# Block 0: norms in one step ahead of the keys, two key scratch tiles, one mask transfer, row copy on ScalarE, earlier query projections

## The chip, the cores and the metric

The kernel runs on one core of a Trainium2 chip. Five engines work side by side, each in the order of its own instruction list: TensorE (PE; its weight loads are shown as PEld), VectorE (DVE), ScalarE (ACT), GpSimd (POOL) and SyncE (SP), which only issues transfers (DMAs). They wait for one another through semaphores. The metric is device time in microseconds (us): the median of 3 runs of the kernel before is 5856.54 us (5856.24 to 5871.77). One execution was also profiled; it took 5850.62 us, with a span of 5848.7 us from first to last instruction.

## The reference

Eight blocks are added to a residual `x` (16 batches x 56 rows x 128 features). The change touches the first alone, `L0_xcond`: six layers of adaptive norm, rotary self-attention, adaptive norm, rotary cross-attention over a context of 1500 keys per batch, adaptive norm, and MLP:

```python
NL, D, H, DFF = (6, 128, 16, 512)          # 16 heads of 8 features
def _adaln(x, emb, w, b):
    g, be = jnp.split(emb[:, 0, :] @ w.T + b, 2, axis=-1)
    return _ln(x) * (1.0 + g[:, None, :]) + be[:, None, :]
def _attn(q, k, v, mask):
    scores = jnp.einsum('bqhd,bkhd->bhqk', q, k) / np.float32(np.sqrt(HD))
    scores = jnp.where(mask[:, None, None, :], -jnp.inf, scores)
    return jnp.einsum('bhqk,bkhd->bqhd', jax.nn.softmax(scores, axis=-1), v)
```

In cross-attention the queries come from the normed state and are rotated (`_rope`), the keys come from the context `ctx` (16 x 1500 x 128) and are rotated too, and the values come from the context unrotated.

## The kernel before, in words

Block 0 (class `Block0`) is one long software pipeline. A **slot** is one batch of cross-attention in one layer; there are 6 x 16 = 96 of them (`NS`), numbered 0 to 95. A slot has 12 **steps** (`kt`), one for each tile of 125 keys. Eight slots make a **phase** (`ph`), which also carries, beside the cross-attention of its eight batches, the MLP of the previous eight batches and the self-attention of the next eight. I count places in a phase from 0 to 7 (slot number modulo 8); `t` counts its 96 steps. All engines walk over the same slots and steps, and each emits its own part of every step in a fixed order, so the tables of step numbers (`T_NORM`, `T_ROPE`, `T_SELF` and others) set where a piece of work stands in every engine's list.

What a step holds:
- TensorE: two groups of four score matmuls (L1561) of the current slot, each followed by one matmul for the row maxima of the next slot (L1575); every second step the weighted sums of values (L1587); at steps 0, 4, 8 a projection of 500 keys (L1601), at steps 2, 6, 10 four projections of values (L1609); at step 10 a transposition of the row maxima, "rows" (L1638). The first scores of a slot wait for the copy of those rows and for the exponentials of step 11.
- ScalarE: two exponentials (L2067) per step, then the key's first bf16 part ("hi", L1966, steps 2, 6, 10), its second part ("mid", L1970, one step later), the value copies (L1987).
- VectorE: the row maxima (L1940), the first half of a key's rotation (L1821, L1822), the copy of the rows into the query stack (L1837, at step 11), the softmax division (L1800 and four L1808).
- GpSimd: a key's rotation (L2087, L2091, one step after the key's projection), then what is left after "hi" (L2094) and after "mid" (L2097), each one step later. The same for queries at steps 1, 3, 5. It also multiplies out the adaptive norms (L2121, L2124, L2126) in two halves, one per step, after the key's work of that step: the MLP norm at t = 9 and 10, the self norm at t = 19 and 20, the cross norm at t = 67 and 68. These are steps 9 and 10 of place 0, and steps 7 and 8 of places 1 and 5.
- SyncE: per slot three sets of 6 key transfers (L1475), 6 mask transfers (L1483), 6 query transfers (L1493) and the fetch of a context.

The norm multiplies wait for ScalarE's inverse root (L2016), emitted one step earlier. The rotated projections ("rope": PE L1698, then four VectorE instructions L1871 to L1879) stand at t = 23 and 24 (self query and key) and 71 (cross query) on TensorE and one step later in VectorE's list. Both ScalarE's "hi" and GpSimd's work are in-order: an instruction that waits holds everything behind it. The scratch tile `tm` (`key_temp`) exists once, so VectorE's work on a key waits for L2097 of the key before.

## Time and profile before

| | us |
|---|---|
| median of 3 runs (range) | 5856.54 (5856.24 to 5871.77) |
| the profiled execution | 5850.62 |
| its span | 5848.7 |
| PE busy | 5394.6 (92%) |
| DVE busy | 4044.0 (69%) |
| ACT busy | 3144.3 (54%) |
| POOL busy | 2240.2 (38%) |

Busy is the time in which an engine executed. Idle time that matters is that of the engine which bounds the stage; a wait of another engine costs only where the first one waits for it in turn. In the rows below an instruction's group shows its start in us from the span's start, its length, and in brackets the idle time of its engine before it and what ended it. A windows row has the stretch and its length, then for PE, PEld, DVE, ACT and POOL the busy time and in brackets the number of instructions, then PEclk (the granted clock of TensorE as a share of 2.4 GHz), the share of the DMA engines that was busy, and GB/s. A group of instructions shows partitions x elements, how many there were, busy us, mean ns of one, and the idle time before them.

### The profile page before, as it was taken

To read this page: it belongs to the slowest core of one execution; us is meant where nothing else is said; L and a number is where in the kernel's file an instruction comes from. 1 tells how busy PE (TensorE), PEld (TensorE's weight loads), DVE (VectorE), ACT (ScalarE), POOL (GpSimd) and SP (SyncE) were. 2 spreads that over 40 slices of the span, in tenths; PEclk is the share of its full clock that TensorE was granted. 3 is DMA by queue.
4 is the path that set the end of the run, shared out by engine and by line. 5 is a ranking of instruction groups with operands and counts; after the bars stand their busy time and mean duration, and the time that the engine had idled before them with its cause. 6 is when DMAs were issued, how large, how long until landed. Compare 5 with 4: busy or idle time off the path is not lost.

```text
span 5848.7 us, 144909 instructions
## 1 busy us (share of the span) xinstructions
PE 5394.6 (92%) x57797; PEld 4270.3 (73%) x57797; DVE 4044.0 (69%) x8355; ACT 3144.3 (54%) x6405; POOL 2240.2 (38%) x2209
## 2 busy tenths in 40 slices
PE   5899999999999999999978999999699999989998
PEld 4667677676776766767645799998389889947984
DVE  3888887888888888888744377776556666644653
ACT  1566666766666667666644333434334334424764
POOL 4665665666666666666500000000011111075440
PEclk8999999999999999999988999999899999998998
DMA  2776776767767777677810011110100000030000
GB/s 63 118 124 100 122 116 108 122 110 117 120 110 120 112 114 123 103 124 116 119 51 20 22 33 33 38 37 13 41 12 12 17 17 12 12 121 11 2 1 26
DMA packets 440503, 408.12 MB, mean 70 GB/s; under 512 B 125576, under 2 KB 420947, under 8 KB 437787
## 3 DMA queue, kind: packets, MB, share of 16 engines
q1 hardware_dynamic: 439834, 398.85, 39.2%
q8 instruction: 463, 7.59, 0.7%
q14 instruction: 206, 1.68, 0.1%
HBM read 158.00 MB, written 0.46 MB: 27 GB/s over the span
## 4 chain that ended last, share of the span: by engine, by line
PE 61%; POOL 8%; DVE 7%; SPq 7%; issue 6%; DMA 5%; ACT 4%; POOLq 1%; DVEq 1%; ACTq 0%
PE psum L2248 10%; PE psum L2278 10%; PE psum L1575 5%; PE psum L1587 4%; PE psum L1561 4%; SPq L1475 3%; POOL slot_context L3547 3%; DMA l_ctx_v<-in_ctxV 3%; PE psum L1609 3%; PE psum L1723 3%; PE psum L1601 2%; PE psum L416 2%; SPq L1493 2%; PE psum L430 2%; DVE row_max L1940 2%
## 5 line engine op out<-in xcount | busy, mean ns | idle before, releaser
L1940 DVE TENSOR_REDUCE row_max<-psum 112x1 f32<-112x500 f32 x2304 | 1443.5, 670 | 187.4 <-PE psum L1575 172.6
L2067 ACT ACTIVATE weights<-psum 125x448 f32<-125x448 f32 x2304 | 1141.3, 541 | 521.7 <-PE psum L1561 515.2
L1575 PE MATMUL psum<-key_stack,query_stack 97*128 97x500 bf16 x2304 | 875.7, 381 | 107.9 <-DMA query_stack<-query_parts 47.9
L1561 PEld LDWEIGHTS psum<-query_stack,key_stack 121*128 121x128 bf16 x9216 | 654.6, 99 | 370.7 <-issue 184.4
L1561 PE MATMUL psum<-query_stack,key_stack 121*128 121x112 bf16 x9216 | 837.9, 213 | 33.5 <-ACT weights L2067 28.0
L2278 PE MATMUL psum<-l_ctx_v,l_weights 125*128 125x129 f32 x5376 | 638.6, 274 | 1.8 <-ACT l_u L2352 1.8
L2278 PEld LDWEIGHTS psum<-l_ctx_v,l_weights 125*128 125x128 f32 x5376 | 618.3, 191 | 2.5 <-issue 2.5
L1587 PE MATMUL psum<-weights,values 125*17 125x112 f32 x18432 | 554.9, 261 | 0.0
L1587 PEld LDWEIGHTS psum<-weights,values 125*17 125x17 f32 x18432 | 408.9, 97 | 144.8 <-issue 140.4
L2097 POOL TENSOR_TENSOR key_parts<-key_temp,key_parts 128x500 bf16<-128x500 f32 x288 | 327.2, 1136 | 421.5 <-ACT key_parts L1970 421.5
L2087 POOL TENSOR_TENSOR key_temp<-key_temp,rope_sin 128x500 f32<-128x500 f32 x288 | 360.5, 1252 | 282.2 <-DVE key_temp L1821 282.2
L2366 ACT ACTIVATE l_weights<-l_weights 125x1536 f32<-125x1536 f32 x224 | 332.4, 1484 | 236.3 <-DVE l_weights L2410 236.3
L2410 DVE TENSOR_TENSOR l_weights<-psum,l_shift 125x1536 f32<-125x1536 f32 x224 | 392.0, 1750 | 97.5 <-ACT l_shift L2344 97.5
L2418 DVE TENSOR_REDUCE l_tile_max<-psum 125x128 f32<-125x1536 f32 x224 | 393.4, 1756 | 67.1 <-PE psum L2248 66.3
L2094 POOL TENSOR_TENSOR key_temp<-key_temp,key_parts 128x500 f32<-128x500 f32 x288 | 328.4, 1140 | 231.9 <-ACT key_parts L1966 231.8
L2091 POOL TENSOR_TENSOR key_temp<-key_temp 128x500 f32<-128x500 f32 x288 | 358.2, 1244 | 42.5 <-POOL key_temp L2087 1.7
L2248 PE MATMUL psum<-l_q,l_keys 128*125 128x128 f32 x2688 | 372.3, 283 | 0.6 <-ACT l_q L2238 0.6
L2336 ACT ACTIVATE l_w<-psum,l_stat 128x128 f32<-128x128 f32 x224 | 82.4, 368 | 534.3 <-DVE l_stat L2400 534.2
L1575 PEld LDWEIGHTS psum<-key_stack,query_stack 97*128 97x128 bf16 x2304 | 224.4, 97 | 172.8 <-DMA query_stack<-query_parts 68.4
L2248 PEld LDWEIGHTS psum<-l_q,l_keys 128*125 128x125 f32 x2688 | 331.6, 194 | 22.0 <-issue 21.1
L2248 PE MATMUL psum<-l_q,l_ctx_t 128*125 128x128 f32 x2688 | 343.8, 273 | 0.6 <-ACT l_q L2238 0.6
L3042 POOL MEMSET l_weights<- 125x128 f32 x2 | 0.4, 216 | 884.4 <-DVE x_state L796 884.4
(549 smaller groups left out, 10227.5 us busy)
## 6 DMA issues: line engine op xcount, KB each, us to landing
key_stack<-key_parts SPq DMA_DIRECT2D x1728, 125.0 KB, 4.6
ctx_t<-in_ctxT SPq DMA_DIRECT2D x96, 750.0 KB
l_ctx_v<-in_ctxV SPq DMA_DIRECT2D x32, 750.0 KB
query_stack<-query_parts SPq DMA_DIRECT2D x576, 28.0 KB, 3.4
l_ctx_t<-in_ctxT SPq DMA_DIRECT2D x16, 750.0 KB
slot_context<-in_ctxV SPq DMA_DIRECT2D x16, 750.0 KB
key_stack<-ctx_mask_rows SPq DMA_DIRECT2D x576, 3.9 KB
sm_w<-in_sm_w SPq DMA_DIRECT2D x3, 2048.0 KB
```

The costliest lines, as they stand in the source:

```text
L1561: mm = e.matmul(self.k.psum[:, h, (p % 4) * QC:(p % 4 + 1) * QC], ks[:, at:at + 128], q[:, p * QC:(p + 1) * QC])
L1575: e.matmul(self.k.psum[:, 2 + n % 2, 0:500], q[0:ROWS_MAX, p * QC:p * QC + 128], ks[0:ROWS_MAX, p, c * 500:(c + 1) * 500]).then_inc(self.m ...
L1587: mm = e.matmul(self.k.psum[32 * j:32 * j + 17, 5, g * QC:(g + 1) * QC], v[:, kt, p, :], w[:, p * QC:(p + 1) * QC], start=kt == 0 and g == ...
L1940: e.tensor_reduce(self.largest[:, i % PAIRS, i // PAIRS:i // PAIRS + 1], k.psum[0:QC, 2 + i % 2, 0:500], AX.X, ALU.max, negate=True).then_ ...
L2067: e.activation(half(self.p[kt % RING_P], h), self.k.psum[0:KN, h, 0:HALF], ACT.Exp).then_inc(self.exped.sem, 1)
L2087: e.tensor_tensor(tm[:, 1, :], tm[:, 1, :], self.sin[:, c * 500:(c + 1) * 500], ALU.mult).then_inc(self.key_turned_sin.sem, 1)
L2091: e.tensor_tensor(tm[:, 0, :], tm[:, 0, :], tm[:, 1, :], ALU.add).then_inc(self.key_rotated.sem, 1)
L2248: mm = e.matmul(self.scores(i)[:, t, :], self.keys(b)[:, t * KN:(t + 1) * KN], q)
L2278: mm = e.matmul(acc, p[:, t, :], v[:, t, :], start=t == 0, stop=t == self.tiles - 1)
L2366: op = e.activation(p[:, 0:KT, :], p[:, 0:KT, :], ACT.Exp)
L2410: e.tensor_tensor(p[:, 0:KT, :], self.scores(j), shift.unsqueeze(1).broadcast_to([KN, KT, 128]), ALU.add).then_inc(self.shifted.sem, 1)
L2418: e.tensor_reduce(self.most, self.scores(i).rearrange("p t q -> p q t"), AX.X, ALU.max).then_inc(self.max_ready.sem, 1)
```

## The change

Six edits, all in Block 0 (and line numbers below them shift by a few):
1. `T_ROPE`: the query projections move from t = 23 to 22 and from 71 to 70. The key projection stays at 24.
2. Each norm's two halves stand in one step (the first of the two), and ahead of the query's and key's work of that step on GpSimd.
3. `tm` becomes two tiles, and the wait of VectorE moves from the key before to the one before that.
4. The copy of the rows moves from VectorE (its step 11, after the steps' phase work) to ScalarE (start of step 11, ahead of the exponentials).
5. The six mask transfers of a slot become one of 8 x 1500 elements; the mask's rows are made once as 16 x 1500 instead of 96 x 250.
6. Two of every four transpositions of the sums are written 8 columns further left, so that the division is one multiply of 56 x 128 instead of four of 56 x 32.

```diff
-T_UP, T_DOWN, T_ROPE, T_SV = {13: (0, 1, 2, 3)}, 15, {23: 0, 24: 1, 71: 2}, 24
+T_UP, T_DOWN, T_ROPE, T_SV = {13: (0, 1, 2, 3)}, 15, {22: 0, 24: 1, 70: 2}, 24
...
-            for n in range(6):
-                e.dma_start(dst[ROWS:ROWS + 1, :, n * 250:(n + 1) * 250],
-                            self.mask_rows[6 * b + n:6 * b + n + 1, :].unsqueeze(1).broadcast_to(
-                                [1, PAIRS, 250])).then_inc(self.mask_stacked.sem, 16)
+            e.dma_start(dst[ROWS:ROWS + 1, :, :],
+                        self.mask_rows[b:b + 1, :].unsqueeze(1).broadcast_to([1, PAIRS, L])).then_inc(
+                            self.mask_stacked.sem, 16)
...
-        for g in range(2):
-            for h2 in range(2):
...
-                op = e.tensor_tensor(o[:, m * 32:(m + 1) * 32].rearrange("p (j d) -> p j d", j=4), v,
-                                     spread(inv[:, 4 * m:4 * m + 4], 8), ALU.mult)
-        op.then_inc(side.emptied(*key), 1)
+        e.tensor_tensor(o.rearrange("p (m d) -> p m d", d=8), bk.rearrange("p (m c) -> p m c", c=32)[:, :, 1:9],
+                        spread(inv, 8), ALU.mult).then_inc(side.emptied(*key), 1)
...
-            if (b, c) > (0, 0):
-                e.wait_ge(self.key_lo.sem, self.key_lo(b, c) - 1)
+            if (b, c) > (0, 1):
+                e.wait_ge(self.key_lo.sem, self.key_lo(b, c) - 2)
...
-    def rows_vector(self, e, b):
+    def rows_scalar(self, e, b):
...
+        e.activation(self.q_stack[b % 3][ROWS:ROWS_ALL, :].rearrange("r (p c) -> r p c", p=PAIRS),
+                     rows.unsqueeze(1).broadcast_to([1 + 3 * PAIRS, PAIRS, QC]), ACT.Copy).then_inc(
+                         self.side.emptied(*key), 1)
...
@@ gpsimd @@
+                ph, t = s // BH, 12 * (s % BH) + kt
+                for name, at in T_NORM.items():
+                    layer = MLP_OF(ph) if name == "mlp" else NEXT_OF(ph)
+                    if layer is not None and t == at + 3:
+                        for h in range(2):
+                            self.norm_gpsimd(e, name, ph, layer, h)
                 if 0 <= s + 2 < NS:
                     self.query_gpsimd(e, s, kt)
                 self.key_gpsimd(e, s, kt)
-                ph, t = s // BH, 12 * (s % BH) + kt
-                for name, at in T_NORM.items():
-                    layer = MLP_OF(ph) if name == "mlp" else NEXT_OF(ph)
-                    if layer is not None and t - at - 3 in range(2):
-                        self.norm_gpsimd(e, name, ph, layer, t - at - 3)
```

GpSimd's list around an MLP norm (steps 8 to 11 of place 0; `x_normed` rows are the norm, `key_temp` and `key_parts` the key, `query_block` is step 1 of the next slot), before:

```order
L2087 TENSOR_TENSOR key_temp<-key_temp,rope_sin 128x500
L2091 TENSOR_TENSOR key_temp<-key_temp 128x500
L2121 TENSOR_TENSOR x_normed<-ln_deviation 128x224
L2124 TENSOR_TENSOR x_normed<-x_normed,adaln_scale_shift 128x224
L2126 TENSOR_TENSOR x_normed<-x_normed,adaln_scale_shift 128x224
L2094 TENSOR_TENSOR key_temp<-key_temp,key_parts 128x500
L2121 TENSOR_TENSOR x_normed<-ln_deviation 128x224
L2124 TENSOR_TENSOR x_normed<-x_normed,adaln_scale_shift 128x224
L2126 TENSOR_TENSOR x_normed<-x_normed,adaln_scale_shift 128x224
L2097 TENSOR_TENSOR key_parts<-key_temp,key_parts 128x500
L2105 TENSOR_TENSOR query_block<-l_q,head_parity 128x112
```

The same place of the changed kernel:

```order
L2115 TENSOR_TENSOR x_normed<-ln_deviation 128x224
L2118 TENSOR_TENSOR x_normed<-x_normed,adaln_scale_shift 128x224
L2120 TENSOR_TENSOR x_normed<-x_normed,adaln_scale_shift 128x224
L2115 TENSOR_TENSOR x_normed<-ln_deviation 128x224
L2118 TENSOR_TENSOR x_normed<-x_normed,adaln_scale_shift 128x224
L2120 TENSOR_TENSOR x_normed<-x_normed,adaln_scale_shift 128x224
L2081 TENSOR_TENSOR key_temp<-key_temp,rope_sin 128x500
L2085 TENSOR_TENSOR key_temp<-key_temp 128x500
L2088 TENSOR_TENSOR key_temp<-key_temp,key_parts 128x500
L2091 TENSOR_TENSOR key_parts<-key_temp,key_parts 128x500
L2099 TENSOR_TENSOR query_block<-l_q,head_parity 128x112
```

The key's rotation (L2087 and L2091 before, L2081 and L2085 now) stood ahead of the norm and now stands behind all six of its multiplies.

ScalarE's list at the same place (inverse root of the norm, the exponentials `weights` of steps 9 and 10, key hi, values, step 11), before:

```order
L2016 ACTIVATE ln_deviation<-ln_deviation 128x224 x2
L2067 ACTIVATE weights<-psum 125x448 x4
L1966 ACTIVATE key_parts<-key_temp 128x500
L1987 ACTIVATE values<-psum 125x32x16
L2067 ACTIVATE weights<-psum 125x448 x2
L1970 ACTIVATE key_parts<-key_temp 128x500
```

and of the changed kernel:

```order
L2008 ACTIVATE ln_deviation<-ln_deviation 128x224 x2
L2061 ACTIVATE weights<-psum 125x448 x4
L1958 ACTIVATE key_parts<-key_temp 128x500
L1979 ACTIVATE values<-psum 125x32x16
L1830 ACTIVATE query_stack<-psum 25x896
L2061 ACTIVATE weights<-psum 125x448 x2
L1962 ACTIVATE key_parts<-key_temp 128x500
```

The row copy (L1830) stands between the key's and values' copies of step 10 and the exponentials of step 11, in every slot.

TensorE's list from the rows of step 10 to the first scores of the next slot, where a query projection (`l_w_attend`) moves, before:

```order
L1638 MATMUL psum<-ident_bf,neg_max_parts 72x112
L1561 MATMUL psum<-query_stack,key_stack 128x112 x4
L1575 MATMUL psum<-key_stack,query_stack 128x500
L1561 MATMUL psum<-query_stack,key_stack 128x112 x4
L1575 MATMUL psum<-key_stack,query_stack 128x500
L1587 MATMUL psum<-weights,values 17x112 x16
L1698 MATMUL psum<-x_normed,l_w_attend 128x448
L1561 MATMUL psum<-query_stack,key_stack 128x112 x4
```

and of the changed kernel:

```order
L1637 MATMUL psum<-ident_bf,neg_max_parts 72x112
L1697 MATMUL psum<-x_normed,l_w_attend 128x448
L1560 MATMUL psum<-query_stack,key_stack 128x112 x4
L1574 MATMUL psum<-key_stack,query_stack 128x500
L1560 MATMUL psum<-query_stack,key_stack 128x112 x4
L1574 MATMUL psum<-key_stack,query_stack 128x500
L1586 MATMUL psum<-weights,values 17x112 x16
L1560 MATMUL psum<-query_stack,key_stack 128x112 x4
```

The projection moved ahead of step 11's scores and maxima; VectorE's four rope instructions move from ahead of the maxima of the next slot's step 0 to ahead of those of step 11.

## Rows read from the trace of the kernel before

**Rows 1.** Windows: slots 32 and 39 (places 0 and 7)
```profile
1118.44:1142.39 23.95, 23.78 (x358) 16.80 (x354) 21.09 (x47) 18.67 (x41) 16.86 (x18) 1.00 0.91 142
1329.35:1356.13 26.78, 23.90 (x353) 16.98 (x349) 21.18 (x45) 17.69 (x38) 16.01 (x16) 0.94 0.92 143
```

**Rows 2.** Waits of PE in Block 0's slots (total us, times, longest us)
```profile
PE psum L1575 <- DMA query_stack<-query_parts: 45.6, 32, 3.5
PE psum L1575 <- DVE row_max L1940: 29.1, 47, 1.4
PE psum L1561 <- ACT weights L2067: 28.0, 38, 1.0
PE psum L1747 <- DVE query_stack L1837: 7.8, 22, 0.4
```

**Rows 3.** Timeline of ACT at an MLP norm, slot 32
```profile
1137.64 0.67 ACT L2016 ACTIVATE ln_deviation<-ln_deviation 128x224 f32<-128x224 f32 x2
1140.09 0.61 ACT L1966 ACTIVATE key_parts<-key_temp 128x500 bf16<-128x500 f32 x1
1141.23 0.97 ACT L2067 ACTIVATE weights<-psum 125x448 f32<-125x448 f32 x2
```

**Rows 4.** Timeline of POOL there
```profile
1137.03 1.27 POOL L2087 TENSOR_TENSOR key_temp<-key_temp,rope_sin 128x500 f32<-128x500 f32 x1 [1.38 <-DVE key_temp L1821]
```

**Rows 5.** Timeline of PE there: first scores of slot 33
```profile
1142.39 0.37 PE L1561 MATMUL psum<-query_stack,key_stack 121*128 121x112 bf16 x4
```

**Rows 6.** Timeline of POOL at a cross norm, slot 29 (place 5)
```profile
1061.55 0.67 POOL L2121 TENSOR_TENSOR x_normed<-ln_deviation 128x224 f32<-128x224 f32 x1
...
1065.36 1.24 POOL L2087 TENSOR_TENSOR key_temp<-key_temp,rope_sin 128x500 f32<-128x500 f32 x1
```

**Rows 7.** Timeline of ACT there
```profile
1068.03 0.62 ACT L1966 ACTIVATE key_parts<-key_temp 128x500 bf16<-128x500 f32 x1 [3.13 <-POOL key_temp L2091]
```

**Rows 8.** Timeline of PE there: first scores of slot 30, and its second step
```profile
1069.71 0.36 PE L1561 MATMUL psum<-query_stack,key_stack 121*128 121x112 bf16 x4 [0.95 <-ACT weights L2067]
...
1072.29 0.39 PE L1575 MATMUL psum<-key_stack,query_stack 97*128 97x500 bf16 x1 [0.56 <-DVE row_max L1940]
```

**Rows 9.** Timeline of DVE there: rope, then row maxima
```profile
1068.80 0.62 DVE L1871 SCALAR_TENSOR_TENSOR l_q<-psum,rope_cos 128x448 f32<-128x448 f32 x1 [0.38 <-PE psum L1698]
...
1071.56 1.26 DVE L1940 TENSOR_REDUCE row_max<-psum 112x1 f32<-112x500 f32 x2
```

**Rows 10.** Timeline of PE at a late query stack, slot 39
```profile
1351.17 0.38 PE L1575 MATMUL psum<-key_stack,query_stack 97*128 97x500 bf16 x1 [2.82 <-DMA query_stack<-query_parts]
```

**Rows 11.** Windows of PE there: us, PE busy, PEclk, DMA share, GB/s
```profile
1352.00:1356.00 4.00, 4.00 (x51) 0.57 1.12 132
```

**Rows 12.** Windows: slot 7, columns as in rows 1
```profile
382.57:410.93 28.36, 24.75 (x352) 17.66 (x349) 21.53 (x45) 17.69 (x38) 15.69 (x16) 0.88 0.93 144
```

**Rows 13.** Groups by line: copies on DVE and ACT
```profile
L1837 DVE COPY query_stack<-psum 25x896 bf16<-25x896 bf16 x95 | 58.7, 618 | 11.3 <-PE psum L1638 7.9
L1987 ACT ACTIVATE values<-psum 125x512 f32<-125x512 f32 x282 | 166.5, 590 | 11.8 <-PE psum L1609 7.5
L1957 ACT ACTIVATE sums<-psum 128x224 f32<-128x224 f32 x95 | 34.0, 358 | 53.1 <-PE psum L1587 53.1
```

**Rows 14.** Timeline of SP, slot 39: mask, keys, queries
```profile
1334.71 4.10 SPq L1483 DMA_DIRECT2D key_stack<-ctx_mask_rows  x6
1338.85 5.25 SPq L1475 DMA_DIRECT2D key_stack<-key_parts  x6
```

**Rows 15.** Timeline of POOL, slot 39: the key that the second SP row waits for
```profile
1337.45 1.14 POOL L2097 TENSOR_TENSOR key_parts<-key_temp,key_parts 128x500 bf16<-128x500 f32 x1 [0.54 <-ACT key_parts L1970]
```

**Rows 16.** Timeline of POOL at the start: making the masks
```profile
58.30 2.45 POOL L2145 TENSOR_SCALAR src_mask<-src_mask 1x896 bf16<-1x896 uint8 x1
60.82 0.86 POOL L2146 TENSOR_SCALAR ctx_mask_rows<-ctx_mask 96x250 bf16<-96x250 uint8 x1
62.95 3.34 POOL L2163 TENSOR_TENSOR l_qd<-l_q,head_of_feature 128x896 f32<-128x896 f32 x2 [1.27 <-DVE l_q L1879]
```

More of the change, by code:

```diff
@@ L1290, in __init__ @@
             self.q_tmp = sb("query_block", [128, 2, QC])
-            self.tm = sb("key_temp", [128, 2, 500])
+            self.tm = [sb(f"key_temp{i}", [128, 2, 500]) for i in range(2)]
             self.ctx_t = [sb(f"ctx_t{i}", [128, L])[:, :] for i in range(2)]
@@ L1616, in fixed_tensor @@
             for i in range(4):
-                tr = e.transpose(side.bank(*key)[0:S, i * 128:(i + 1) * 128], self.acc[:, i * S:(i + 1) * S],
-                                 k.ident[:, :])
+                at = i * 128 - 8 * (i % 2)
+                tr = e.transpose(side.bank(*key)[0:S, at:at + 128], self.acc[:, i * S:(i + 1) * S], k.ident[:, :])
             tr.then_inc(side.filled, 1)
@@ L1933, in vector @@
                     self.max_parts_vector(e, s + 1)
-                if 0 <= s + 1 < NS and kt == 11:
-                    self.rows_vector(e, s + 1)
                 if self.max_at(s, kt):
@@ L2062, in scalar @@
             for kt in range(KT):
+                if 0 <= s + 1 < NS and kt == 11:
+                    self.rows_scalar(e, s + 1)
                 for h in range(2 if 0 <= s < NS else 0):
@@ L2074, in key_gpsimd @@
     def key_gpsimd(self, e, s, kt):
-        tm, side = self.tm, self.side
+        side = self.side
         for late in range(1, 4):
@@ L2083, in key_gpsimd @@
             b, c = at
-            part = self.k_part[(3 * b + c) % 2]
+            part, tm = self.k_part[(3 * b + c) % 2], self.tm[(3 * b + c) % 2]
             if late == 1:
```

31 lines of the change are left out of this document (13 added, 18 removed).

## The prediction, made before the changed kernel ran

> **What bounds the kernel now.** I first took the page's busy shares, then the waits of TensorE in Block 0, then windows cut at each slot's first score matmul, and last the timelines of the places where the diff moves something. Block 0's slots run from 178.9 to 2963.7 us of the span; nothing behind that is touched. Slots repeat by their place in the phase: those with much self-attention last about 34 us, those without about 24 us. In a short slot TensorE is busy nearly throughout, 23.78 of 23.95 us in slot 32, where slot 39 has 23.90 of 26.78 [rows 1]. So TensorE sets the pace, and a change can win only TensorE's waits or create new ones. The waits are in rows 2: 45.6 us for the query stack's transfer, 29.1 us for VectorE's row maxima, 28.0 us for ScalarE's exponentials, 7.8 us that end when VectorE's row copy lets it go on. With a few smaller ones that is some 120 us, 2% of the time, and the most that can be won. The other engines each have room (DVE 21 of 24 us, ACT 19, POOL 17 in slot 32), yet all are in-order, so what matters is which instruction stands behind which wait.
>
> **Part 1, the MLP norm ahead of the key's rotation (my main term).** At step 9 of place 0, GpSimd rotated the key first: L2087 starts at 1137.03 [rows 4], before the norm's inverse root is ready (L2016 runs from 1137.64 to 1138.31 [rows 3]). Now all six norm multiplies stand ahead of it. They start when the root's first half is there, about 1138.1. The six take 3.81 us from the first to the start of the next instruction (1061.55 to 1065.36 [rows 6]), and from L2087's start to the start of ScalarE's key copy that waits for it are 2.67 us (1065.36 to 1068.03 [rows 6, 7]). That puts the key copy at 1138.1 + 3.81 + 2.67 = 1144.6, where it stood at 1140.09 [rows 3]. The copy is in-order on ScalarE, which had come to it by 1140.1: it now waits 4.5 us, and behind it are the values' copy, the row copy and the two exponentials of step 11, for which the next slot's first scores wait. The trace has this wait at place 5, where the norm already stood in front of a rotation: ScalarE waited 3.13 us there [rows 7] and the scores came 1.68 us after the copy's start, 0.95 us late (1068.03 to 1069.71 [rows 7, 8]). Here the row copy comes on top, 0.84 us (part 3): 1144.6 + 1.68 + 0.84 = 1147.1, against 1142.39 [rows 5]. A stall of 4.7 us, once in each MLP phase that still has keys to make, which are the phases starting at slots 8, 16, ... 88: 11 x 4.7 = **+51.7**.
>
> A stall of TensorE also costs clock. After a wait of 2.82 us for a query stack [rows 10] the granted clock over the next 4 us was 0.57 [rows 11], that is partly at the lower of its two levels, 1.2 GHz: 0.43 x 4 = 1.7 us lost. After the 3.5 us wait of slot 7 [rows 2] it was 0.88 over 28.36 us [rows 12], 3.4 us lost. A stall of 4.7 us is longer than each of these, so I take the smaller loss every time: 11 x 1.7 = **+18.7**; ends 0 and 11 x 3.4 = 37. The Trainium skill (TensorE: Matmul & The Clock Gate, "HAM oscillation") says of loops in which the array sits idle for a transfer that the clock falls to half and that matmuls after the wait pay for it; the trace agrees in rows 10 and 11, and the rule speaks against this change. Without it the sum would be 18.7 us lower.
>
> **Part 2, the self and cross norms.** At places 1 and 5 the norm moves ahead of L2097 of the key before, which was waiting anyway, and so out of the way of the next key's rotation. By the same steps the ScalarE wait of 3.13 us shrinks to about 1 and TensorE's 0.95 us at the next slot's start to 0.2. That occurs 22 times: 22 x 0.75 = **-17** of the 28.0 us.
>
> **Part 3, the row copy on ScalarE.** VectorE took 618 ns for it. ScalarE's time for 896 elements is not in the trace: from 224 elements in 358 ns and 512 in 590 ns [rows 13] it is 590 + 384 x 0.81 = 0.90 us, of which about 0.84 hold the next instruction. Its ends are 0.62 (VectorE's own) and 1.11 (the 1.24 ns per element of a key copy, 0.62 us for 500 [rows 3]). It stands ahead of step 11's exponentials. In a short slot the first of these ends at about 1141.77 (1141.23 and half of 0.97 [rows 3]) and TensorE comes for it at 1142.39 [rows 5]: 0.62 of slack, less an estimated 0.14 for the handover from engine to engine. So the copy exceeds it by 0.36 us. In long slots TensorE has more to do there and it is hidden. Places 6 and 7 pay, and the last slots, 26 in all: 26 x 0.36 = **+9** (ends 0 and 16). What VectorE gives up frees the 7.8 us wait: **-7**.
>
> **Part 4, rope one step sooner.** Four rope instructions hold VectorE 2.76 us (1068.80 to 1071.56 [rows 9]), in front of maxima for which TensorE soon waits: 0.56 us now [rows 8]. One step sooner they stand right behind step 10's five small instructions on the maxima and ahead of step 11's; TensorE may run two maxima ahead and then waits, I work out about 1.1 us at the next slot's step 0, for each of the 22 moved ropes: +24. The 0.56 goes (11 times, -6), as does a part of the other 36 waits for row maxima (29.1 - 6.2 = 23 us [rows 2]): I take 8 us for those at step 10, where VectorE's key no longer waits for L2097. Net **+10** (ends -14, where all of the row-maxima waits at these places go, and +24). This step is the weakest of the sum.
>
> **Part 5, queries and masks.** The 45.6 us occur at places 6 and 7. The six mask transfers hold SyncE 4.1 us, one would hold 0.7. But what stands behind them waits for GpSimd: in slot 39 the key was ready at 1338.59 [rows 15], the mask transfers ended at 1338.81 and the key's began at 1338.85 [rows 14], so only 0.25 us come of the 3.4. At place 6 the rope no longer stands between VectorE and that slot's first new key: by the 2.76 us less what part 4 charges, the key comes over 1 us sooner. I take 1 us at 11 places 6 and 0.25 at 12 places 7: **-14** (ends 0 and -45.6; if the longest waits go, clock losses like those of rows 11 and 12 go with them, 2 to 3 us each).
>
> **Part 6, the rest.** The one multiply for four, 0.2 us on VectorE per division, and the second `key_temp` lie beside TensorE's work in the steady slots; their cover is VectorE's room of some 3 us a slot, and their gain is in the terms above. At the start the serial chain of masks and keys is bare: one mask transfer saves up to 3.4 us of SyncE; making the mask takes GpSimd longer, (2.45 - 0.86)/646 elements = 2.5 ns each, so 0.86 + 1250 x 2.5 ns = 3.9 us instead of 0.86, of which 1.27 was idle before the next instruction [rows 16] and most of the rest is covered by the key's rope. Net **-2** (ends -6 and +2).
>
> **Sum.** 51.7 + 18.7 - 17 + 9 - 7 + 10 - 14 - 2 = +49 on the profiled execution's own 5850.6, so 5900. The median of the runs shown lies 5.9 above that execution: 5905.
>
> **The rivals.**
> - *The stall is partly given back, no change.* ScalarE and GpSimd catch up while TensorE stands still, so later waits of place 1 vanish, and the clock stays up. Stall worth 2.2 us net: 11 x 2.2 = 24, with the other terms (-21) 5853.6, median 5859. For it: place 1 is long and full of small waits. Against: TensorE sets the pace in every slot, so it can give back only waits of its own, and rows 2 divided by 96 slots leave little more than 1 us in each.
> - *Faster.* The key's rotation isn't held: by some slack that I miss, ScalarE's key copy at step 10 isn't in front of anything that TensorE needs, and the earlier ropes cost nothing. Then parts 1 and the +24 go: 49 - 70 - 24 = -45, 5805.6, median 5812. It would decide where the copy's start comes before about 1140.6 + 0.5. Against it speak rows 7 and 8, where the same wait did reach TensorE.
> - *Slower still.* The clock falls as in slot 7 after every stall, and the row copy takes 1.11 us: 49 + 18.7 + 7 = 75, median 5931.
> - *The change doesn't do what it says.* The query stack is not sooner, since SyncE waits for GpSimd; only part 5's 14 us hang on it, and the time would be 5919, within the forecast.
>
> **How the numbers follow.** Forecast 5905 with 0.61 (its own range 5872 to 5930), given back 0.18, faster 0.13, slower still 0.08. What a measurement can tell from no change is about 0.3%, 17.6 us: 5839 to 5874. Faster holds 0.13; same 0.18 and the forecast's low tail of 0.03; slower the rest, 0.66. The range goes from 5843, which leaves out the faster case and little else, to 5935, which takes in the longer clock loss.
>
> **What the new profile would show.** Right: POOL's norm rows directly behind the inverse root at place 0, six in a row, and then the key's rotation; an ACT key copy there with some 4 us of idle before it, put down to POOL; PE's first scores of slots 9, 17, ... 89 with over 4 us idle and a lower PEclk behind; at places 2 and 6 the 0.95 us gone and a row-maxima wait of about 1 us at step 0; ACT's row copy at 0.9 us; the query waits still near 30 us. Wrong: no idle above 1 us at slots 9, 17, ...; the forecast then has nothing left that makes the kernel slower, and the time falls to the faster case.

## The result: 5866 us, 0.2% slower, and the profile after

The changed kernel takes 5866.25 us (median of 12 runs, 5854.87 to 5886.98); the kernel before took 5855.70 in the same comparison (12 runs, 5843.07 to 5871.77). The ratio is 1.0023, 95% interval 1.0013 to 1.0032: slower by 11 us, where I had forecast 49. The sign and the range hold; the size doesn't.

I cut both traces at Block 0's first and last score. The columns are those of [rows 1], first the kernel before, then the changed one:

```profile
178.93:2963.70 2784.77, 2646.52 (x37768) 1924.60 (x37772) 2281.26 (x5170) 1890.33 (x4098) 1699.88 (x1693) 0.99 0.72 114
2963.70:5844.60 2880.90, 2641.60 (x19469) 2272.91 (x19468) 1689.57 (x3017) 1219.83 (x2236) 450.62 (x441) 0.94 0.09 26
```

```profile
177.08:2989.50 2812.42, 2652.55 (x37768) 1934.61 (x37772) 2181.87 (x4525) 1977.88 (x4193) 1700.18 (x1693) 0.98 0.72 113
2989.50:5855.60 2866.10, 2626.97 (x19469) 2261.57 (x19468) 1689.26 (x3014) 1219.44 (x2236) 450.11 (x441) 0.95 0.09 27
```

Block 0 is 27.6 us longer. The code behind it, which nobody touched, is 14.8 us shorter: in both, TensorE idles 239 us there, and only its busy time differs (more on this at the end). A second execution of the changed kernel (changed_again, below) puts Block 0 at 24.9 us longer and the rest at 5.6 us shorter. The traces thus put the cost in Block 0 at 25 to 28 us, above the 11 us of the medians; the kernel before was traced once, so no run says which is nearer. In Block 0, VectorE is busy 99 us less and ScalarE 88 us more.

The waits of TensorE in Block 0 after the change, for [rows 2]:

```profile
PE psum L1560 <- ACT weights L2061: 96.5, 76, 5.2
PE psum L1574 <- DMA query_stack<-query_parts: 35.9, 28, 4.2
PE psum L1574 <- DVE row_max L1932: 8.7, 28, 0.7
```

The wait for exponentials grew from 28.0 to 96.5 us; 53 us of that are at place 1, where I had forecast 51.7. But the wait for row maxima fell from 29.1 to 8.7, and the one for the query stack by 10; the row copy's 7.8 are gone. Added over the phases, slots at place 0 grew by 49 us and at place 1 by 17; places 2 to 5 together shrank by 43.

The place of the forecast stall, slot 32, now shows ScalarE (answers to [rows 3]) ...

```profile
1142.70 0.67 ACT L2008 ACTIVATE ln_deviation<-ln_deviation 128x224 f32<-128x224 f32 x2
1143.28 1.97 ACT L2061 ACTIVATE weights<-psum 125x448 f32<-125x448 f32 x4
1149.63 0.62 ACT L1958 ACTIVATE key_parts<-key_temp 128x500 bf16<-128x500 f32 x1 [4.39 <-POOL key_temp L2085]
1150.16 0.58 ACT L1979 ACTIVATE values<-psum 125x512 f32<-125x512 f32 x1
1150.76 0.91 ACT L1830 ACTIVATE query_stack<-psum 25x896 bf16<-25x896 bf16 x1
1151.69 0.98 ACT L2061 ACTIVATE weights<-psum 125x448 f32<-125x448 f32 x2
```

... GpSimd (to [rows 4]), the norm's first multiply and the key's rotation behind it ...

```profile
1143.17 0.68 POOL L2115 TENSOR_TENSOR x_normed<-ln_deviation 128x224 f32<-128x224 f32 x1 [2.47 <-ACT ln_deviation L2008]
...
1146.98 1.24 POOL L2081 TENSOR_TENSOR key_temp<-key_temp,rope_sin 128x500 f32<-128x500 f32 x1
```

... TensorE (to [rows 5]), the first scores of slot 33, and the 4 us from there as a window:

```profile
1152.38 0.53 PE L1560 MATMUL psum<-query_stack,key_stack 121*128 121x112 bf16 x4 [4.86 <-ACT weights L2061]
```

```profile
1152.40:1156.40 4.00, 4.00 (x18) 2.21 (x19) 1.93 (x4) 1.96 (x5) 1.46 (x2) 0.50 0.14 36
```

The six norm multiplies take 3.81 us, the key copy idles 4.39 us, TensorE 4.86, and then runs at the lower of its two clock levels. That is part 1 as forecast (4.7 us, then clock). The rule that the prediction cited from the Trainium skill (TensorE: Matmul & The Clock Gate, "HAM oscillation") fits this window too, though the loops it speaks of wait for a transfer and here TensorE waits for ScalarE. What I had not forecast is at the start of place 6, slot 30 (to [rows 8]):

```profile
1074.92 0.36 PE L1560 MATMUL psum<-query_stack,key_stack 121*128 121x112 bf16 x4 [1.17 <-ACT weights L2061]
1075.57 0.39 PE L1574 MATMUL psum<-key_stack,query_stack 97*128 97x500 bf16 x1 [0.29 <-DVE row_max L1932]
```

The 0.95 us did not shrink to 0.2, it is 1.17; and the wait for maxima is 0.29 us, not 1.1.

### The profile page after: what moved, and what is told of

Read it like the earlier page. It is cut to its first block, busy times and chain, and to the rows that moved or that the text cites. A ratio compares the mean times of both kernels' runs of the same rounds, so it can differ in the third digit from the quotient of the medians.

```text
span 5859.8 us, 143852 instructions
## 1 busy us (share of the span) xinstructions
PE 5383.4 (92%) x57797; PEld 4267.4 (73%) x57797; DVE 3942.6 (67%) x7683; ACT 3232.3 (55%) x6501; POOL 2243.0 (38%) x2209
## 4 chain that ended last, share of the span: by engine, by line
PE 66%; POOL 8%; issue 6%; ACT 5%; DMA 5%; DVE 4%; SPq 3%; POOLq 1%; DVEq 0%; ACTq 0%
PE psum L2243 10%; PE psum L2273 10%; PE psum L1574 6%; PE psum L1560 6%; PE psum L1586 6%; PE psum L1600 3%; PE psum L1608 3%; POOL slot_context L3542 3%; DMA l_ctx_v<-in_ctxV 3%; PE psum L1722 2%; PE psum L416 2%; PE psum L430 2%; SPq L1475 2%; SPq L1492 1%; ACT weights L2061 1%
## 5 line engine op out<-in xcount | busy, mean ns | idle before, releaser
L1560 PEld LDWEIGHTS psum<-query_stack,key_stack 121*128 121x128 bf16 x9216 | 662.3, 100 | 451.5 <-issue 159.3
L1560 PE MATMUL psum<-query_stack,key_stack 121*128 121x112 bf16 x9216 | 844.5, 214 | 102.5 <-ACT weights L2061 96.5
L2091 POOL TENSOR_TENSOR key_parts<-key_temp,key_parts 128x500 bf16<-128x500 f32 x288 | 326.9, 1135 | 449.4 <-ACT key_parts L1962 449.4
L2081 POOL TENSOR_TENSOR key_temp<-key_temp,rope_sin 128x500 f32<-128x500 f32 x288 | 360.4, 1251 | 216.8 <-DVE key_temp L1814 216.8
L2085 POOL TENSOR_TENSOR key_temp<-key_temp 128x500 f32<-128x500 f32 x288 | 357.7, 1242 | 42.7 <-POOL key_temp L2081 2.2
L2901 POOL TENSOR_TENSOR l_ctx_v<-l_ctx_v,l_ctx_w 125x512 f32<-125x512 f32 x48 | 56.8, 1183 | 719.5 <-DVE l_ctx_v L2895 719.5
```

Of the source, the lines that this page charges most:

```text
L1560: mm = e.matmul(self.k.psum[:, h, (p % 4) * QC:(p % 4 + 1) * QC], ks[:, at:at + 128], q[:, p * QC:(p + 1) * QC])
L2081: e.tensor_tensor(tm[:, 1, :], tm[:, 1, :], self.sin[:, c * 500:(c + 1) * 500], ALU.mult).then_inc(self.key_turned_sin.sem, 1)
L2085: e.tensor_tensor(tm[:, 0, :], tm[:, 0, :], tm[:, 1, :], ALU.add).then_inc(self.key_rotated.sem, 1)
```

## The experiments

All medians are of 4 to 12 runs, but for the last row. The kernel before ran beside each of them (medians 5850.6 to 5856.0), and the ratio is to those runs. A difference to before is taken from the ratio or from those medians, which agree within 5 us. "Block 0" is the stretch between its first and last score in the profiled execution.

| run | median us | ratio to before (95%) | Block 0 us |
|---|---|---|---|
| before | 5855.7 | | 2784.8 |
| changed | 5866.3 | 1.0013 to 1.0032 | 2812.4 |
| mlp_norm_back | 5795.8 | 0.9886 to 0.9913 | 2739.2 |
| norms_as_before | 5833.7 | 0.9951 to 0.9978 | 2780.8 |
| rows_on_vector | 5902.5 | 1.0066 to 1.0093 | 2834.1 |
| rope_back | 5882.4 | 1.0033 to 1.0058 | 2820.4 |
| one_key_temp | 5950.7 | 1.0148 to 1.0175 | 2886.7 |
| mlp_back_one_temp | 5878.7 | 1.0028 to 1.0058 | 2819.5 |
| masks_six | 5899.3 | 1.0064 to 1.0090 | 2839.9 |
| division_in_four | 5880.0 | 1.0031 to 1.0057 | 2806.1 |
| rows_ahead_of_hi | 5796.6 | 0.9893 to 0.9921 | 2742.4 |
| before_norms_ahead | 5975.8 | 1.0189 to 1.0217 | 2907.8 |
| before_two_temps | 5848.2 | 0.9982 to 1.0006 | 2782.3 |
| before_self_cross_two_temps | 5863.5 | 1.0008 to 1.0036 | 2788.4 |
| before_rows_on_scalar | 5874.6 | 1.0026 to 1.0058 | 2816.6 |
| before_rope_sooner | 5869.2 | 1.0011 to 1.0037 | 2795.2 |
| before_rows_and_rope | 5884.7 | 1.0030 to 1.0067 | 2809.9 |
| before_one_mask | 5829.4 | 0.9946 to 0.9976 | 2770.6 |
| before_four_joined | 5853.9 | 0.9992 to 1.0015 | 2778.9 |
| changed_again | 5869.7 (1 run) | | 2809.7 |

### The MLP norm: my main term

**mlp_norm_back** (changed kernel):

```diff
 for name, at in T_NORM.items():
-    if layer is not None and t == at + 3:
+    if name != "mlp" and layer is not None and t == at + 3:
...
 self.key_gpsimd(e, s, kt)
+if MLP_OF(ph) is not None and t - T_NORM["mlp"] - 3 in range(2):
+    self.norm_gpsimd(e, "mlp", ph, MLP_OF(ph), t - T_NORM["mlp"] - 3)
```

> The changed kernel with one part undone: the MLP norm's halves stand again behind the key's and query's work, one at t = 9 and one at t = 10; the self and cross norms stay at one go and in front. Theory A (the stall is a cost of its own): the places 0 and 1 of the phases, 66 us longer in the trace of the changed kernel than in that of the kernel before, return to 24.5 and 33.8 us a slot, the 4.5 to 5.6 us of idle ahead of the first scores of slots 9, 17, ... 89 vanish, and the time falls by 55 to 70 us against the changed kernel, to about 5800, below the kernel before. Rival B (the shortening of places 2 to 5 by 42 us is only what the engines gain while TensorE stands in the stall): those places grow again, and the time falls by 25 us at most, to about 5840. Rival C (loss and gain lie in what the trace happened to catch): within 10 us of the changed kernel.

70.4 us faster than the changed kernel, 59 faster than the one before. Theory A holds: places 0 and 1 return (270 and 362 us over the eleven phases from slot 8 on, from 318 and 386), and places 2 to 5 stay as short as they were (371, 358, 334, 287; changed 369, 358, 334, 287), which refutes B. Its waits of TensorE:

```profile
PE psum L1560 <- ACT weights L2061: 48.9, 76, 1.2
PE psum L1574 <- DMA query_stack<-query_parts: 34.0, 29, 3.4
PE psum L1574 <- DVE row_max L1932: 7.6, 24, 0.8
```

And its Block 0, to be read against the changed kernel's row above:

```profile
179.00:2918.20 2739.20, 2628.85 (x37768) 1922.52 (x37772) 2182.02 (x4525) 1973.54 (x4193) 1698.82 (x1693) 1.00 0.73 116
```

TensorE's idle time in Block 0 is 110.4 us, against 159.9 in the changed kernel: 49.5 us for a forecast of 51.7. Its busy time is 23.7 us less, and I had 18.7 for the clock. So part 1 is worth what it was forecast at, and all the rest of the change takes off 59 us, where I had 21. By the traces, 46 us of these are in Block 0 (28 idle time of TensorE and 18 busy time) and 11 in the untouched code. The question is where these come from.

**before_norms_ahead** (kernel before, with the new loop of the norms alone):

> The kernel before with one part of the change alone: all norm halves in one step and ahead of the query's and key's work on GpSimd; everything else as before. Theory A: the stall at place 0 costs 66 to 70 us; what the self and cross norms give back is at most the 17 us of my part 2; so 49 to 70 us above the kernel before, 5905 to 5925. Rival B (given back in places 2 to 5 by the stall itself): 25 us above, about 5880. My part 2 as put on record would show as TensorE's idle at the starts of places 2 and 6 falling from 0.95 to 0.2 us; its rival is that it doesn't move.

121 us slower than the kernel before by the medians (5854.7 in that comparison). Neither theory had that. Its waits:

```profile
PE psum L1575 <- DVE row_max L1940: 98.5, 53, 2.5
PE psum L1575 <- DMA query_stack<-query_parts: 49.7, 31, 4.0
PE psum L1561 <- ACT weights L2067: 43.6, 27, 4.1
```

Beside the stall stand 98.5 us for row maxima (29.1 before). A norm in front makes GpSimd late with a key; with one scratch tile VectorE can't begin the next key, and the maxima stand behind that key. That is my reading here; the next two runs test it.

### The second key_temp

**one_key_temp** (changed kernel) and **mlp_back_one_temp** (the same with the MLP norm back):

```diff
-self.tm = [sb(f"key_temp{i}", [128, 2, 500]) for i in range(2)]
+self.tm = [sb("key_temp", [128, 2, 500])] * 2
...
-if (b, c) > (0, 1):
-    e.wait_ge(self.key_lo.sem, self.key_lo(b, c) - 2)
+if (b, c) > (0, 0):
+    e.wait_ge(self.key_lo.sem, self.key_lo(b, c) - 1)
```

> The changed kernel with one key_temp again: VectorE's work on a key waits for L2097's counterpart of the key just before. My part 6 and part 3 of the prediction: this lies beside TensorE's work; within 5 us of the changed kernel (5866). Theory now: with the norms in front, a key's parts leave GpSimd up to 4 us later at places 0, 1 and 5, and with one scratch tile VectorE's next key waits for that, with the row maxima behind it; norms moved in the kernel before cost 121 us, with TensorE's waits for row maxima at 104 us against 35, where the changed kernel loses only 66 us to the same move. So the second tile is worth 30 to 50 us there: 5895 to 5915, the waits for row maxima rise from 9 to over 40 us, at places 1, 5 and 6.

> The changed kernel with the MLP norm back and one key_temp. With both norms in front and one tile the changed kernel was at 5951, with two at 5866, and with the MLP norm back and two tiles at 5796. Theory (the tile's 84 us belong to the norms in front, at places 1, 5 as at 0): without the MLP norm two of the three places remain, 22 of 33, and the tile is worth 56 us: 5852. Rival (only the MLP norm's 4 us make VectorE wait): within 15 us of 5796. Second rival (the tile is worth the same 84 everywhere): 5880. The waits for row maxima would be 70, 20 and 100 us.

84 us slower with the MLP norm in front, 83 without. The mechanism of my theory stands, its place was wrong: the MLP norm has no part in it. TensorE waits 2.5 us for maxima at each place 1 and 5 and 1.5 at 2 and 6 in both. One wait also covers another: with the maxima late, ScalarE's exponentials are in time more often. The second run's rows, to be read against those of mlp_norm_back:

```profile
PE psum L1574 <- DVE row_max L1932: 98.5, 79, 2.5
PE psum L1574 <- DMA query_stack<-query_parts: 30.2, 27, 2.7
PE psum L1560 <- ACT weights L2061: 21.6, 48, 0.5
```

**before_two_temps** and **before_self_cross_two_temps**: the tile alone on the kernel before, and with it the self and cross norms in front.

> The kernel before with the second key_temp alone. Prediction: it frees up to 8 us of waits for row maxima (part 4) and is hidden otherwise: 5845 to 5855. Rival (VectorE's wait for L2097 is what makes its row maxima late at places 1, 2, 5 and 6): the waits for row maxima fall from 35 to under 15 us, 20 to 30 us faster, 5825 to 5835. Second rival: nothing, since the tile matters only where a norm stands in front.

> The kernel before with the second key_temp and the self and cross norms at one go in front; the MLP norm as before. Prediction: parts 2 and the 8 us of part 4: -17 - 8 = 25 us faster, 5830. Rival (the norms in front pay only with the second tile, and the pair carries most of the 59 us): 40 to 60 us faster, about 5805. Second rival (they pay only with the row copy off VectorE too): within 10 us of before.

The tile alone: no difference that can be told. With the norms: 13 us slower than before, 15 slower than the tile alone, so neither my -17 nor the first rival; the second (within 10 us of before) is nearest. The wait for exponentials did fall as part 2 said, 35.0 to 7.1 us. But waits for maxima and for keys took most of its place:

```profile
PE psum L1575 <- DMA query_stack<-query_parts: 44.3, 32, 3.3
PE psum L1575 <- DVE row_max L1940: 25.5, 24, 2.0
PE psum L1575 <- DMA key_stack<-key_parts: 18.8, 10, 2.3
...
PE psum L1561 <- ACT weights L2067: 7.1, 16, 0.4
```

Even so TensorE idles 5 us less in Block 0 than with the tile alone (130.5 against 135.4). It is busy 11 us longer (2657.9 against 2646.9), and the clock records show 10 us more lost to the lower level: waits that come in longer pieces cost clock as well.

### Part 2 in the changed kernel

**norms_as_before** (changed kernel, the loop of the norms as it was):

> The changed kernel with all norm halves back: two steps, behind the key's and query's work, the self and cross norms too. Against the run with only the MLP norm back (5796), this tells part 2 by itself. Part 2 of the prediction (self and cross norms in front gain 17 us): 5813, and TensorE's idle for exponentials at the starts of places 2 and 6 grows from 1.17 to about 1.9 us each. Rival (the idle of 1.17 us there is the wait of the key copy behind the norm plus the row copy of 0.9 us, and the norm's place moves nothing in the sum): within 5 us of 5796. Second rival: the norm's first half now waits in front where it did not, and undoing it gains: 5785.

38 us slower than mlp_norm_back. Undone, TensorE's idle for exponentials is 2.6 us at the start of nearly every place 2 and 6, against 1.17. Among the other edits the norms in front gain 38 us; on the kernel before, with the tile alone beside them, they cost 15.

### Row copy and ropes

**rows_on_vector** and **rope_back** (changed kernel, one edit undone each):

> The changed kernel with the row copy back on VectorE, at its place behind the phase work of step 11. Part 3 of the prediction (copy on ScalarE costs 9, frees 7): 2 us faster, within 5 us either way. Rival: the copy in front of step 11's exponentials is why TensorE's 0.95 us at the starts of places 2 and 6 did not go (1.2 us now) and why places 6 and 7 are 3 us longer in all, and it lengthens the stall at place 1 by 0.8 us: 22 x 1 + 11 x 0.8 = 30 us faster, less the 8 us of waits behind the row copy that return, some 20 us. Second rival: VectorE's relief gave the 42 us of places 2 to 5; then slower by 10 to 20 us.

> The changed kernel with the query projections back at t = 23 and 71. Part 4 of the prediction (earlier ropes cost 10 us): the time falls by 10 us (ends: rises 14, falls 24). Revised theory, after the traces: waits of TensorE for row maxima fell from 29.1 to 8.7 us and places 2 and 3 and 5 got shorter by 1 us a slot, and it is the earlier rope that did it; then the time rises by 15 to 30 us, the waits for row maxima return to 20 us or more, at places 2 and 6 above all. Rival: VectorE's relief by the row copy, the division and the second scratch tile did it; then within 5 us.

36 and 16 us slower; both of my terms had the wrong sign here. With the copy on VectorE the first scores (L1560) wait for it, because the ropes stand ahead of it in VectorE's list:

```profile
PE psum L1560 <- ACT weights L2060: 49.0, 29, 4.1
PE psum L1560 <- DVE query_stack L1830: 38.6, 22, 1.8
```

But the sum of TensorE's idle time in Block 0 is the same, 158.4 us here and 159.9 in the changed kernel. What grew is its busy time, by 23 us:

```profile
178.60:3012.70 2834.10, 2675.69 (x37770) 1940.68 (x37773) 2244.47 (x4621) 1890.74 (x4099) 1699.91 (x1693) 0.98 0.71 112
```

The idle at the starts of places 2 and 6 is 1.75 us here and 1.17 in the changed kernel. The first 4 us of slot 30, here and in the changed kernel:

```profile
1089.69:1093.69 4.00, 3.66 (x17) 2.01 (x18) 2.89 (x6) 1.09 (x2) 0.70 (x2) 0.61 1.07 255
```

```profile
1074.92:1078.92 4.00, 3.71 (x54) 2.25 (x54) 3.84 (x8) 2.76 (x6) 2.16 (x3) 1.00 1.08 232
```

The granted clock is 0.61 in the one and 1.00 in the other. By the clock records the lower level falls into 14 of the 24 slots at places 2 and 6 here, mostly at 1.7 us lost each, and into none of the changed kernel's. The same holds for other runs: 17 slots in norms_as_before (idle 2.6 us at these starts), 15 in before_rope_sooner (1.75), 10 in before_rows_on_scalar (2.0), but at most 2 wherever that idle is 0.9 to 1.3 us. TensorE's busy time in Block 0 is 23 us longer here than in the changed kernel, 19 longer in norms_as_before than in mlp_norm_back, 9 longer in before_rope_sooner than before (2 in before_rows_on_scalar). So a good part of the first three prices is clock, which no list of waits shows.

With the ropes back, a part of the waits moves to the keys' transfer:

```profile
PE psum L1574 <- DMA key_stack<-key_parts: 17.0, 10, 2.0
PE psum L1574 <- DVE row_max L1932: 15.1, 25, 1.7
```

**before_rows_on_scalar**, **before_rope_sooner**, **before_rows_and_rope** (kernel before, one edit or both):

> The kernel before with the row copy on ScalarE alone. Part 3 of the prediction: +9 - 7 = 2 us slower than before (5857). Rival, after the run that put it back on VectorE in the changed kernel and lost 36 us: VectorE's 0.62 us and its wait for the rows stood in front of row maxima that TensorE needs; 20 to 35 us faster, places 2 to 5 shorter, the wait of 7.8 us gone and the waits for row maxima below 20. Second rival: the 36 us come only together with the sooner ropes, which otherwise stand in front of VectorE's row copy; then within 8 us of before.

> The kernel before with the query projections at t = 22 and 70 alone. Part 4 of the prediction without the share that the second key_temp has: +24 - 6 = 18 us slower. Rival, after the run that put them back in the changed kernel and lost 16 us: 10 to 20 us faster. Second rival (the ropes now stand ahead of VectorE's row copy at step 11, for which the next slot's first scores wait; with the copy on VectorE the changed kernel waited 47 us for it): 20 to 45 us slower, seen as TensorE's idle for the row copy at the starts of places 2 and 6.

> The kernel before with the row copy on ScalarE and the ropes one step sooner. Alone they cost 24 and 14 us. Theory of a pair (the sooner ropes cost because they stood ahead of VectorE's row copy, 31 us of waits for it; with the copy gone from there the rope's part turns to a gain of about 15): 24 - 15 = 9 us slower, 5865. Additive: 38 slower, 5893. Prediction's own terms: +2 and +18, 20 slower.

The row copy alone is 24 us slower, the ropes alone 14, and both together 28. The ropes alone are close to my 18, but not for my reason: the waits for maxima, which I had growing, fell from 29.1 to 19.1 us, and 23.1 us of waits for VectorE's row copy came instead. The row copy alone I had at 2. Its waits:

```profile
PE psum L1561 <- ACT weights L2068: 64.4, 68, 2.0
PE psum L1575 <- DMA query_stack<-query_parts: 63.5, 38, 3.6
PE psum L1575 <- DVE row_max L1939: 22.6, 58, 1.7
```

The copy stands behind a late key copy on ScalarE; I had looked at places 6 and 7 only, and "hidden in long slots" was wrong for the starts of places 2 and 6 (2.0 and 1.8 us of idle there, 0.95 before). The query stack's wait grows by 18 us too; why, no run isolates.

### The mask transfer and the division

**masks_six** (changed kernel) and **before_one_mask** (kernel before); the diff is the one shown of L1483, backwards and forwards.

> The changed kernel with six mask transfers a slot again, and the mask's rows 96 x 250. Part 5 of the prediction gives the one transfer 0.25 us at 12 places 7, that is 3 us, and part 6 some 2 us at the start: 5 us slower. Rival: SyncE's 3.4 us a slot bring every set of queries and keys sooner; TensorE's waits for the query stack go back from 36 to 46 us or more: 10 to 20 us slower. Second rival: nothing, within 3 us.

> The kernel before with the one mask transfer alone. Parts 5 and 6 of the prediction give it 3 + 2 = 5 us: 5850. Rival, after the run that undid it in the changed kernel and lost 33 us with TensorE's waits for the query stack at 72 instead of 36 us: SyncE's time counts at places 5, 6, 7 and 0, and the kernel gets 15 to 35 us faster, with the waits for the query stack falling from 46 to under 30. Second rival: nothing, since SyncE waits for GpSimd there.

33 us slower and 23 us faster, where I had 5. The wait for the query stack is 71.5 us against 35.9 in the one pair, 33.1 against 45.6 in the other:

```profile
PE psum L1575 <- DMA query_stack<-query_parts: 71.5, 43, 4.7
```

```profile
PE psum L1574 <- DMA query_stack<-query_parts: 33.1, 28, 3.1
```

I had taken the gain from slot 39, where GpSimd's key held it to 0.25 us [rows 14, 15]. In slot 38, a place 6, SyncE's list looks otherwise. First the kernel before, whose slot starts at 1304.52, then the one with one mask transfer, whose slot starts at 1308.73:

```profile
1310.39 5.21 SPq L1483 DMA_DIRECT2D key_stack<-ctx_mask_rows  x6
1315.65 2.59 SPq L1475 DMA_DIRECT2D key_stack<-key_parts  x4
```

```profile
1314.62 0.70 SPq L1482 DMA_DIRECT2D key_stack<-ctx_mask_rows  x1
1319.12 3.15 SPq L1475 DMA_DIRECT2D key_stack<-key_parts  x5
```

The key's transfers follow the masks at once in the first (11.13 us into the slot), and come 10.38 us into it in the second: 0.75 us sooner, where I had given the mask 0.25 us at place 7 and nothing at place 6. Nor is place 6 where most of the wait goes. On the kernel before it falls from 4.9 to 1.0 us at place 0 and from 21.5 to 19.2 at place 7. In the changed kernel it is 12.1 us at place 5 with six transfers and 1.4 with one, 29.6 and 19.0 at place 7, 8.7 and 1.7 at place 0. By Block 0 alone the transfer gives 14 us on the kernel before and 27 in the changed one.

**division_in_four** (changed kernel):

> The changed kernel with the division as four multiplies of 56 x 32 and the transpositions at multiples of 128 columns. Prediction, part 6: hidden, within 3 us. Rival: VectorE was the engine that held TensorE's row maxima, and each of its 0.2 us per division counts in part, 192 divisions in the phases: 5 to 15 us slower, seen in the waits for row maxima at places 2 to 5.

14 us slower by the median, but not in Block 0, which is 6 us shorter (4 us against changed_again). The stretch behind it has 2889.20 us instead of 2866.10, with the same instructions:

```profile
178.70:2984.80 2806.10, 2652.17 (x37768) 1933.08 (x37772) 2216.87 (x5074) 1977.65 (x4193) 1701.12 (x1693) 0.99 0.72 113
2984.80:5874.00 2889.20, 2649.20 (x19469) 2278.88 (x19468) 1689.44 (x3017) 1219.44 (x2236) 449.90 (x441) 0.94 0.09 26
```

So I read the division as hidden in Block 0, as forecast; whether the 14 us belong to it is open.

### All together

**before_four_joined** (kernel before with tile, self and cross norms, row copy and ropes):

> The kernel before with four edits at once: second key_temp, self and cross norms at one go in front, row copy on ScalarE, ropes one step sooner; MLP norm, masks and division as before. Theory (each takes away the wait that another creates): the changed kernel with the MLP norm back is at 5796; less the mask's 23 to 33 us and the division's 0 to 14 this is 5820 to 5843, that is 10 to 30 us faster than before. Additive rival (-4 + 17 + 28, from the runs of one or two edits): 41 us slower, 5893. Prediction's terms (-17 + 2 + 10 = -5): 5847.

3 us above before, within the measurement. The additive rival (5893) falls, and so does my theory of a gain of 10 to 30. Its waits:

```profile
PE psum L1575 <- DMA query_stack<-query_parts: 67.2, 44, 3.5
PE psum L1561 <- ACT weights L2068: 44.1, 79, 1.2
PE psum L1575 <- DVE row_max L1939: 11.6, 23, 1.2
```

The four edits take 17 us of waits for maxima and the row copy's 8 away, and pay it back as 16 for exponentials and 22 for the query stack. Its Block 0, with 140.6 us of idle TensorE:

```profile
180.50:2959.40 2778.90, 2638.34 (x37768) 1930.65 (x37771) 2219.35 (x5074) 1979.47 (x4193) 1699.21 (x1693) 0.99 0.73 114
```

Only mask and division separate this kernel from mlp_norm_back, which is 58 us faster (40 in Block 0), with 34.0 us of waits for the query stack instead of 67.2. The division has at most 14 us of that, so the mask transfer is worth more behind the four edits than alone.

**rows_ahead_of_hi** (mlp_norm_back, with the row copy at step 10, ahead of the key copy, at places 1 and 5):

```diff
-if 0 <= s + 1 < NS and kt == 11:
+if 0 <= s + 1 < NS and kt == 11 and s % BH not in (1, 5):
     self.rows_scalar(e, s + 1)
...
+if 0 <= s + 1 < NS and kt == 10 and s % BH in (1, 5):
+    self.rows_scalar(e, s + 1)
 self.fixed_scalar(e, s, kt)
```

> The version with the MLP norm back (5796 us), and at places 1 and 5 the row copy stands at step 10 ahead of the key's first copy, instead of at the start of step 11. In the trace of that version, in slot 29, ScalarE waits 1.81 us for GpSimd ahead of the key copy at 1055.22, the rows are there at 1054.2, and the row copy of 0.90 us runs at 1056.35, behind the key copy and the values. Theory: the copy moves into the idle time, and TensorE's 1.17 us at the starts of places 2 and 6 falls to about 0.3: 22 x 0.87 = 19 us faster, 5777, and somewhat more if less of the lower clock follows. Rival (VectorE's row maxima, which TensorE waits 0.29 us for right behind, are the next bound): those waits grow to over 1 us and the time stays within 6 us of 5796.

Nothing gained: the rival holds. The wait changes its name, from exponentials (48.9 to 25.4) to maxima (7.6 to 30.9):

```profile
PE psum L1574 <- DVE row_max L1932: 30.9, 24, 1.4
PE psum L1560 <- ACT weights L2061: 25.4, 55, 0.9
```

**changed_again** (the changed kernel, profiled a second time):

> The changed kernel, a second profile. Block 0 lasted 2812 us in the first, the code behind it 2866 us. If the differences of single traces in Block 0 are the edits' own, it comes to 2812 again, within 5 us; if the code behind differs by the clock alone, it lies between 2866 and 2889 us, and it is 2705 to 2709 us plus the time lost to the lower clock.

Block 0 repeats within 3 us (2809.7), the stretch behind it only within 9 (2875.3). One repetition can't prove it, but it suggests that differences of Block 0 above some 5 us are the edits' own. What TensorE lost behind Block 0 to the lower clock, summed from the trace's clock records within the stretch, is 164.0 us, and 2875.3 less that is 2711.3. That is 2 us above the expected 2705 to 2709; the first trace of the changed kernel has 2711.7 by the same sum, division_in_four 2707.5.

The best version measured is mlp_norm_back, with rows_ahead_of_hi equal to it: 1.0% below the kernel before and 1.2% below the changed one.

## Why the forecast was too high

- **Part 1 was right**, in mechanism, place and size: 4.86 us for 4.7 in slot 32; in all 70.4 us (undoing it) for 70.4. That the last digit agrees is luck: the medians it comes from are good to several us, and Block 0 gives 71 to 73. The rival "given back" is refuted for it: places 2 to 5 are as short without the stall.
- **The step that failed is the sum of the other parts**: -21 forecast, -59 to -60 measured (5795.8 against 5855.7, or 5854.7 in its own comparison). Block 0 shows 46 of them; the other 11 are in untouched code, so the edits' own may be less. I priced each edit on the trace of before, alone, and added up. Even the true single prices would not have done: measured on the kernel before, tile, self and cross norms (beside the tile), row copy with ropes, and mask come to -4 + 15 + 28 - 23 = +16.
- **Clock outside part 1 was put at nothing.** I priced the clock for the stall alone. At the starts of places 2 and 6 it decides much of what undoing a single edit costs: 23 us with the copy back on VectorE, where the idle time did not grow at all.
- **Part 5 is the one term that was too small in both kernels**: the mask transfer, 3 us in part 5 and 2 in part 6, measured 23 alone and 33 in the changed kernel (14 and 27 by Block 0). I generalised from one slot of place 7, and "the 45.6 us occur at places 6 and 7" was misread: 31 of them do, the rest lies at the other places, 4.9 us at place 0. "Query waits still near 30 us" came near all the same (35.9), without being the sign that I took it for.
- **Part 4**: near in number for the ropes alone (14 measured for 18), by luck, as the wait was another one. In the changed kernel they gain 16. Beside the row copy alone on the kernel before they add 4 us (28 against 24), so the gain needs more than the copy's move. The +24 rested on a wait for maxima of 1.1 us that is 0.29.
- **Part 3**: the copy's duration was right (905 ns for 0.90), its cover was not: 24 for 2 us alone. In the changed kernel it gains 36, since it takes the copy from behind the ropes, and the lower clock goes with that wait.
- **Part 2**: the cause was right, the price not: 38 for 17 us beside the other edits (42 in Block 0, of which 23 are idle time of TensorE), a loss of 15 without row copy and ropes. Its 0.95 us seemed not to move, because the row copy put back what the norm gave.
- **Part 6**: the second tile was called hidden. It is, where nothing makes GpSimd late (4 us, not to be told from nothing); with norms in front it carries 83 us. The 2 us at the start can't be told: Block 0's first score comes at 178.93 us before and at 177.08 and 178.61 in the two traces of the changed kernel, and between 178 and 185 in the other runs.

What joins the edits is seen at the starts of places 2 and 6. Three chains end there together: GpSimd, key copy, exponentials; VectorE's ropes, row copy, maxima; SyncE's queries. Cutting one shows the next one. Shown is that the waits change names at nearly equal sums (TensorE idles 138 us in Block 0 before, 141 with four edits, 110 with mask and division on top), and that the clock follows how long the single wait is. That the sum is held by just these three chains is my reading of it.

## What to carry to other kernels

When several in-order engines reach one point within a microsecond of each other, the price of an edit isn't a property of the edit: ask for each which wait is next, and price the set. For a resource that several slots share, read its slack at every place of the period, not at one. And a move ahead on an in-order engine is charged with everything it passes: this one, the MLP norm's, could be charged within a few us from the rows of the kernel before, and should have been left out. Last, count a wait's clock with it: two kernels with equal idle time differ by 23 us here.

## What was not expected of the hardware

The code behind Block 0 is the same in every kernel here, and TensorE idles 234 to 242 us in it in all traces, yet it lasted from 2866 to 2889 us. In two executions of the changed kernel it lasted 2866 and 2875. The difference is TensorE's busy time, 2627 us in the changed kernel and 2649 with the division in four; summed from the clock records, the time lost to the lower level is 154 and 182 us in these two. Where the low stretches fall on the same instructions differs from one trace to the next. That is up to 23 us, twice the difference that this case is about, and no trace shows an edit as its cause; only medians of many runs, or the length of the changed stretch alone, could tell the edits apart.
